# Inter-chunk products of a Mamba-style scan as 64x64 quarter products on an unpadded state

## What is computed

```python
def step(state, inp):
    x_t, b_t, c_t, dt_t = inp
    decay = jnp.exp(dt_t * a)[..., None, None]
    b_bar = dt_t[..., None] * b_t
    state = decay * state + b_bar[..., None] * x_t[:, :, None, :]
    y_t = jnp.einsum('bhn,bhnp->bhp', c_t, state)
    return (state, y_t)
...
b = (x @ Wb.T).reshape(bsz, seq, HEADS, STATE)
c = (x @ Wc.T).reshape(bsz, seq, HEADS, STATE)
dt = jax.nn.softplus(x @ Wdt.T + b_dt)
y = _ssd_scan(xh, b, c, dt, a)
y = y + d_param[None, None, :, None] * xh
```

## Time and profile before

| | us |
|---|---|
| median of 3 runs | 1465.38 |
| lowest, highest | 1464.57, 1468.33 |
| the profiled execution | 1465.41 |
| its span in the trace | 1463.4 |
| TensorE busy | 1403.8 (96%) |
| VectorE busy | 996.6 (68%) |
| granted TensorE clock, mean | 0.988 |

### The profile page before, as it was taken

The page is one execution under the profiler, slowest core; times in us unless marked ns, Lnnn a source line. Parts: engine busy times, 40 slices in busy tenths (PEclk is TensorE's granted clock), DMA queues, the critical chain, the costliest instruction groups (busy, mean ns, idle before and its releaser), DMA issues.

```text
span 1463.4 us, 23472 instructions
## 1 busy us (share of the span) xinstructions
PE 1403.8 (96%) x8803; PEld 862.6 (59%) x8803; DVE 996.6 (68%) x2849; ACT 689.1 (47%) x1351; POOL 308.5 (21%) x386
## 2 busy tenths in 40 slices
PE   8999999999999999999999999999999997999984
PEld 4447645676457665576456764576655763567543
DVE  2426797477874787477974778747874779747682
ACT  4443543645455562635436454555626354462312
POOL 3004201341104301142013411043011420133110
PEclk9999999999999999999999999999999998999998
DMA  8000001020000100020010200001000200101010
GB/s 299 10 0 30 15 15 48 3 75 29 26 23 17 61 30 26 22 78 15 15 48 2 76 30 26 22 18 61 29 26 22 77 15 15 47 4 46 29 48 4
DMA packets 47552, 54.24 MB, mean 37 GB/s; under 512 B 7625, under 2 KB 42313, under 8 KB 47441
## 3 DMA queue, kind: packets, MB, share of 16 engines
q1 hardware_dynamic: 41424, 46.41, 9.5%
q0 software_dynamic: 6016, 6.35, 1.7%
HBM read 34.84 MB, written 17.85 MB: 36 GB/s over the span
## 4 chain that ended last, share of the span: by engine, by line
PE 85%; DVE 8%; issue 4%; ACT 1%; POOL 1%; DMA 0%; POOLq 0%; SPq 0%; DVEq 0%
PE ps L1563 41%; PE ps L1729 8%; PE ps L1678 5%; PE ps L1637 4%; PE ps L1630 4%; DVE yst L1166 3%; PE ps L1690 2%; PE ps L1649 2%; PE ps L1869 2%; PE ps L1879 2%; PE ps L1664 2%; PE ps L1655 2%; PE ps L1668 1%; PE ps L1834 1%; PE ps L1800 1%
## 5 line engine op out<-in xcount | busy, mean ns | idle before, releaser
L1563 PE MATMUL ps<-xT,wb_s 128*128 128x512 f32 x512 | 232.9, 601 | 3.6 <-ACT xT L722 3.5
L1563 PE MATMUL ps<-xT,wc_s 128*128 128x512 f32 x512 | 225.4, 593 | 0.0
L1563 PEld LDWEIGHTS ps<-xT,wc_s 128*128 128x128 f32 x512 | 96.1, 190 | 112.3 <-issue 111.9
L1563 PEld LDWEIGHTS ps<-xT,wb_s 128*128 128x128 f32 x512 | 94.1, 191 | 113.1 <-issue 104.5
L1047 DVE SCALAR_TENSOR_TENSOR xT<-xc,cols_s,xT 128x512 f32<-128x512 f32 x192 | 134.8, 748 | 2.7
L1563 PE MATMUL ps<-hT,wx_s 128*128 128x512 f32 x256 | 117.7, 603 | 1.6 <-ACT hT L680 1.2
L1563 PE MATMUL ps<-hT,wz_s 128*128 128x512 f32 x256 | 112.8, 593 | 0.1
L1729 PE MATMUL ps<-CT,xT 128*128 128x256 f32 x512 | 111.9, 379 | 0.9 <-DVE xT L1226 0.9
L747 ACT ACTIVATE BT<-ps 128x512 f32<-128x512 f32 x64 | 37.9, 592 | 150.4 <-PE ps L1563 150.4
L1729 PEld LDWEIGHTS ps<-CT,xT 128*128 128x128 f32 x512 | 97.2, 190 | 17.8 <-issue 5.0
L788 ACT ACTIVATE XB<-ps 128x512 f32<-128x512 f32 x64 | 38.3, 599 | 138.0 <-PE ps L1649 138.0
(11 more groups left out here) (299 smaller groups left out, 2637.5 us busy)
## 6 DMA issues: line engine op xcount, KB each, us to landing
xr<-x SPq DMA_DIRECT2D x8, 1024.0 KB, 9.2
x_scratch<-xr SPq DMA_DIRECT2D x32, 256.0 KB, 2.1
out<-EC SPq DMA_DIRECT2D x32, 256.0 KB, 2.1
BT<-x SPq DMA_DIRECT2D x7, 1024.0 KB, 5.6
modrow<-mod_scratch SPq DMA_DIRECT2D x8, 512.0 KB, 6.6
w_s<-w SPq DMA_DIRECT2D x2, 1024.0 KB, 11.5
BT<-x SPq DMA_DIRECT2D x2, 512.0 KB, 5.2
xT<-wmod SPq DMA_DIRECT2D x1, 1024.0 KB, 9.4
```

The costliest lines, as they stand in the source:

```text
L1563: ins = t_.matmul(bank[:, :], w[:, k, m * P:(m + 1) * P], rhs[:, k, half * HALF:(half + 1) * HALF], start=k == 0, stop=k == nk - 1)
```

## The change

- The state is kept without its zero quarters: `Sst` is 128 partitions by 4 tiles by 64 columns. The inter-chunk product becomes 8 products of 64 rows by 64 columns, each 128 tokens long.
- In tiles 1 and 3 the two heads' state rows are swapped: head `hh` of an odd tile has its state rows in the other half of the partitions. So the quarter products of an even tile go from rows 0 to 63 to output partitions 0 to 63, and from 64 to 127 to 64 to 127; those of an odd tile cross over. The swap of B, C and dt is made in the order of the weights that the host passes.
- y lies in two banks: even tiles in bank 4, columns 0 to 255, odd tiles in bank 5, columns 256 to 511. The state's own products use columns 0 to 255 of bank 5.
- Since y and the state's products share bank 5, TensorE's `state(c)` also waits for `y_ready`, and VectorE's `state(c)` waits for `y_filled` in chunk 0 too.
- VectorE's `state` is one instruction of 128 partitions by 256 instead of two of 64 by 256. GpSimd's decay works on 128x256 instead of 128x512. Two memsets of VectorE per sequence and two of GpSimd in the setup are gone.

```diff
+        def y_tile(k, rows=slice(0, P)):
+
+            o = (k % 2) * 2 * P + (k // 2) * P
+            return ps[4 + k % 2][rows, o:o + P]
...
-        Sbd = sb("Sbd", [P, KC, P])
-        Sdc = sb("Sdc", [P, KC, P])
+        Sst = sb("Sst", [P, KC, STATE])
+        Sdc = sb("Sdc", [P, KC, STATE])
...
-                    g.tensor_tensor(Sdc[:, :, :], Sbd[:, :, :], dec[:, :, c:c + 1].broadcast_to([P, KC, P]),
+                    g.tensor_tensor(Sdc[:, :, :], Sst[:, :, :], dec[:, :, c:c + 1].broadcast_to([P, KC, STATE]),
...
                 def state(c):
                     dve.wait_ge(s_filled, at(s_filled, b, c + 1))
                     if c:
-                        if c or later(b):
-                            dve.wait_ge(Sdc_ready, at(Sdc_ready, b, c))
-
-                        dve.wait_ge(y_filled, at(y_filled, b, c + 1))
-                    for hh in range(2):
-                        q = slice(64 * hh, 64 * hh + 64)
-                        src = ps[5][q, :].rearrange("p (k n) -> p k n", k=KC)[:, :, q]
-                        if c:
-                            ins = v.tensor_tensor(Sbd[q, :, q], src, Sdc[q, :, q], ALU.add)
-                        else:
-                            ins = v.tensor_copy(Sbd[q, :, q], src)
+                        dve.wait_ge(Sdc_ready, at(Sdc_ready, b, c))
+                    dve.wait_ge(y_filled, at(y_filled, b, c + 1))
+                    src = ps[5][:, 0:HALF // 2].rearrange("p (k n) -> p k n", k=KC)
+                    if c:
+                        ins = v.tensor_tensor(Sst[:, :, :], src, Sdc[:, :, :], ALU.add)
+                    else:
+                        ins = v.tensor_copy(Sst[:, :, :], src)
...
-                v.memset(Sbd[0:64, 0, 64:128], 0.0)
-                chS(dve, b, v.memset(Sbd[64:128, 0, 0:64], 0.0))
...
                     for k in range(KC):
-                        t_.matmul(ps[4][:, k * P:(k + 1) * P], Sbd[:, k, :], ECv[:, k, c * P:(c + 1) * P],
-                                  start=k == 0, stop=True, skip_group_check=k > 0)
+                        for r in range(2):
+                            q = slice(64 * r, 64 * r + 64)
+                            hh = (r + k) % 2
+                            t_.matmul(y_tile(k, slice(64 * hh, 64 * hh + 64)), Sst[q, k, :],
+                                      ECv[q, k, c * P:(c + 1) * P], start=k < 2, stop=True,
+                                      skip_group_check=k >= 2)
...
                     if c or later(b):
                         pe.wait_ge(S_ready, at(S_ready, b, c))
-                    for h in range(HEADS):
-                        r, o = slice(64 * (h % 2), 64 * (h % 2) + 64), slice(h * 64, h * 64 + 64)
-                        ins = t_.matmul(ps[5][r, o], XB[:, c % 2, 1, o], XB[:, c % 2, 0, o], start=True, stop=True)
+                        pe.wait_ge(y_ready, at(y_ready, b, c))
+                    for k in range(KC):
+                        for r in range(2):
+                            hh = (r + k) % 2
+                            o, x = k * P + 64 * r, k * P + 64 * hh
+                            ins = t_.matmul(ps[5][64 * r:64 * r + 64, k * STATE:(k + 1) * STATE],
+                                            XB[:, c % 2, 1, o:o + STATE], XB[:, c % 2, 0, x:x + STATE],
+                                            start=True, stop=True)
```

More of the change, by code:

```diff
@@ L44 @@
 SD_MOD, SD_MIX, SD_ALL = 11, 13, 17
-SP_ALL = 46
+SP_ALL = 44
 DT_FLOOR = 2.0 ** -60
-CHAINS = {"A": 4, "V": 9, "D": 7, "S": 4, "G": 20, "R": 45}
+CHAINS = {"A": 4, "V": 9, "D": 7, "S": 3, "G": 20, "R": 45}
 PER_BATCH = {}
@@ L266, in adaln_block @@
         vz = ftmp[:, 3:5, :].rearrange("p a n -> p (a n)").rearrange("p (h n) -> p h n", h=FH)
-        msel = Sbd[:, 0, :]
+        msel = Sst[:, 0:2, :].rearrange("p a n -> p (a n)")
         junk = oT_
@@ L547, in _ @@
             link(g.memset(phase[:, 1, 1, :], PI / 2))
-            link(g.memset(Sbd[:, :, :], 0.0))
-            link(g.memset(Sdc[:, :, :], 0.0))
             link(g.memset(boff[:, :], 0.0))
@@ L1158, in skip @@
                         s = xT[:, k, c * P:(c + 1) * P]
-                        ins = v.scalar_tensor_tensor(s, s, cols_s[:, k, 5:6], ps[4][:, k * P:(k + 1) * P],
-                                                     ALU.mult, ALU.add)
+                        ins = v.scalar_tensor_tensor(s, s, cols_s[:, k, 5:6], y_tile(k), ALU.mult, ALU.add)
                     ins.then_inc(y_ready, 1)
@@ L1636, in output @@
                     k, hh = h // 2, h % 2
-                    ins = t_.matmul(ps[4][64 * hh:64 * hh + 64, k * P:(k + 1) * P],
+                    r = (hh + k) % 2
+                    ins = t_.matmul(y_tile(k, slice(64 * hh, 64 * hh + 64)),
                                     XB[:, c % 2, 0, h * STATE:(h + 1) * STATE],
-                                    Mt[:, c % 2, hh * HALF + k * P:hh * HALF + (k + 1) * P],
+                                    Mt[:, c % 2, r * HALF + k * P:r * HALF + (k + 1) * P],
                                     start=c == 0, stop=True, skip_group_check=c > 0)
@@ L2018 @@
     rep = INNER // HEADS
+    heads = [2 * k + (r + k) % 2 for k in range(KC) for r in range(2)]
+    states = np.concatenate([np.arange(h * STATE, (h + 1) * STATE) for h in heads])
     columns = np.concatenate([
@@ L2025 @@
         "x": arr("L0_attn_input_tensor"),
-        "wxT": arr("L0_attn_Wx").T, "wzT": arr("L0_attn_Wz").T, "wbT": arr("L0_attn_Wb").T,
-        "wcT": arr("L0_attn_Wc").T, "wdtT": np.pad(arr("L0_attn_Wdt").T, ((0, 0), (0, 32 - HEADS))),
+        "wxT": arr("L0_attn_Wx").T, "wzT": arr("L0_attn_Wz").T, "wbT": arr("L0_attn_Wb")[states].T,
+        "wcT": arr("L0_attn_Wc")[states].T,
+        "wdtT": np.pad(arr("L0_attn_Wdt")[heads].T, ((0, 0), (0, 32 - HEADS))),
         "woT": arr("L0_attn_Wout").T, "cols": by_partition(columns),
-        "bdt": np.tile(np.pad(arr("L0_attn_b_dt"), (0, 32 - HEADS)), 4)[:, None], "loga": arr("L0_attn_log_a"),
+        "bdt": np.tile(np.pad(arr("L0_attn_b_dt")[heads], (0, 32 - HEADS)), 4)[:, None],
+        "loga": arr("L0_attn_log_a")[heads],
         "mask": arr("L0_ffn_attention_mask").reshape(MB * L, L),
```

## The result

| | us |
|---|---|
| forecast | 1441.0 (1438 to 1457) |
| measured, median of 4 runs | 1443.74 (1441.15 to 1446.76) |
| before, median of 4 runs beside them | 1465.54 (1464.57 to 1468.33) |
| ratio, with 95% interval | 0.985 (0.983 to 0.988) |
| the same kernel again, 5 more runs (first experiment) | 1441.69 (1439.80 to 1445.84) |

The profiled execution is the slowest of the four: 1446.76, span 1444.9. So between the two traces the difference is 18.5, and between the medians 21.8 and 24.0.

A forecast was written before the change was run, and what follows sets the result against it. TensorE was taken to bound the scan, its matmul groups abutting for a whole chunk. 48 x 0.50 = 24.0 plus VectorE's 0.4 gave 24.4 off 1465.41, so 1441.0 us, range 1438 to 1457.

The forecast's parts named there:

- The length of the group: TensorE's inter-chunk product: 4 turns (0.43) plus a fixed part of 0.16 give 0.59 us instead of 1.09.
- Four side by side: In the inter-chunk product the array takes four quarter passes at once, 0.50 us less per group; chance 0.72.
- Two wide: Rival for the inter-chunk product: 8 turns, 1.02 us per group, gain 3.8, total 1461.6; chance 0.13.
- How often it counts: Inter-chunk products of chunks 1 to 6 are on the chain: 48 of 56, 24.0 us; chunk 7's count nothing.
- VectorE's 0.44, once: VectorE's `state` goes from 0.86 to 0.42; the 0.44 comes out only in the last sequence, where TensorE waits 1.12.
- The added waits: TensorE's `state(c)` on `y_ready` (0.85 ahead at `state(5)`) and VectorE's copy in chunk 0: cost nothing.
- GpSimd: GpSimd's L572 halves from 1.05, with 129 us of idle ahead of it and 1% of the chain: nothing gained.
- The idle ahead of the group-norm matmul: Sign at the end of each scan: TensorE's idle ahead of gn_stats' matmul grows from 0.25 to about 0.75.
- cutting it only adds 0.50: Cutting `output(7)`, beside VectorE's statistics, adds 0.50 to TensorE's idle of 0.25 and gains nothing in all 8 sequences.
- The sum: Whole kernel: 24.0 from TensorE plus 0.4 from VectorE is 24.4, from 1465.41 to 1441.0 us.

The follow-up runs named there:

- first experiment: The changed kernel run again with no edit, as a control: median 1441.69 us, 0.983 of the kernel before.
- second set: Changed kernel with the inter-chunk products of chunks 1 to 6 issued twice, one set right behind the other: 1464.99 us, 0.998 of the kernel before.
- the two doublings: Changed kernel with inter-chunk products issued twice, in chunks 1 to 6 (1464.99 us, 0.998 of before) or in chunk 7 alone (1441.35 us, 0.982).
- a trace that starts and ends as the one before: Trace of the changed kernel with only chunk 7's inter-chunk products issued twice: span 1439.4, median 1441.35 us, 0.982 of the kernel before.

## Why the prediction was right, point by point

- **The length of the group.** Forecast 0.59, measured 0.60. The reading of the earlier trace rows, that a group is so many turns of 0.108 plus a fixed part, held, and it held in the other forms that ran: 8 turns 1.02, two times 4 turns 1.03 (second set 0.43 = 4 x 0.108).
- **Four side by side.** That no row showed a cut in rows and columns at once was the largest open point; the sum took four, and four it was. "Two wide", a gain of 3.8, is what the kernel without the swap gave: 2.4 in the median (1463.28 against 1465.66), and 3.4 in its trace from the mark of sequence 0 to that of sequence 7.
- **How often it counts.** 48 and not 56: shown by the two doublings.
- **VectorE's 0.44, once.** The last sequence gave 3.5, of which 2.94 are TensorE's. The rest is 0.54, not 0.44. The rows of the kernel after (compare):

```profile
1325.81 0.43 DVE L1148 TENSOR_TENSOR Sst<-ps,Sdc 128x256 f32<-128x256 f32 x1 [2.02 <-PE ps L1638]
1326.15 1.11 DVE L1158 SCALAR_TENSOR_TENSOR xT<-xT,cols_s,ps 128x128 f32<-128x128 f32 x4
...
1327.32 0.67 PE L1629 MATMUL ps<-EC,Sst 64*64 64x128 f32 x16 [0.56 <-DVE xT L1158]
```

  and of the kernel before the row behind its `state` at 1345.53:

```profile
1346.42 1.12 DVE L1159 SCALAR_TENSOR_TENSOR xT<-xT,cols_s,ps 128x128 f32<-128x128 f32 x4
```

  The forecast set the lengths of the rows against each other, 0.86 and 0.42. What counts is when skip can start: 0.89 behind `state` before (1346.42 - 1345.53) and 0.34 after (1326.15 - 1325.81), 0.55 less. So the wait fell from 1.12 to 0.56 and not to 0.7. What the sum did not say either is that the shorter instruction keeps the added wait from biting in the other sequences: with it in two instructions, 0.18 of a period is lost.
- **The added waits.** Nothing, as forecast, but the margin was put at 0.85 and is 1.1. The 0.11 by which VectorE's saving was too small counts twice in it.
- **GpSimd.** Nothing, as forecast. Its decay did not halve from 1.05 (it takes 0.62), but it is off the chain.
- **The idle ahead of the group-norm matmul.** Forecast "about 0.75", measured 0.55. The step that failed is "cutting it only adds 0.50": `output(7)` did not become 0.50 shorter. TensorE's timeline before (two rows that the forecast did not use) and after:

```profile
666.19 1.98 PE L1563 MATMUL ps<-hT,wx_s 128*128 128x512 f32 x4
...
669.00 1.09 PE L1637 MATMUL ps<-Mt,XB 128*64 128x128 f32 x16
```

```profile
658.20 1.98 PE L1559 MATMUL ps<-hT,wx_s 128*128 128x512 f32 x4
660.11 0.67 PE L1629 MATMUL ps<-EC,Sst 64*64 64x128 f32 x16
660.71 1.09 PE L1638 MATMUL ps<-Mt,XB 128*64 128x128 f32 x16
```

  From the projection ahead of it to the intra-chunk product it was 669.00 - 666.19 = 2.81 and is 2.51: 0.30 less, which takes the idle from 0.25 to 0.55. The padded product took only 0.99 there (668.01 to 669.00), not 1.09, and the quarters start 0.09 later than it did (1.91 after the projection's start instead of 1.82). A reading that fits, not tested by itself: ahead of `output(7)` stands a full 128x128 matmul, the padded product had that shape too, and the quarters change it; in the loop the neighbour ahead has 64 columns, so both forms pay for a change. It costs nothing here since the place is beside VectorE.
- **The sum.** 1441.0 against 1443.74 and 1441.69. Of the 24.4, a trace that starts and ends as the one before shows 24.0 (1463.4 to 1439.4): 48 x 0.49 + 0.55 = 24.1. Two small errors stood against each other, 0.50 for 0.49 and 0.44 for 0.55. What the forecast left out is that the start and the last feed-forward part vary from one execution to the next; in the profile of the changed kernel they lost 3.7 and 1.8.

## What to carry to other kernels

A product on a block-diagonal operand uses the array for zeros. Cutting it helped here only because the pieces land on different row and column parts of the array at once; arranging the data so that every second tile crosses over (here by permuting weights ahead of time) was worth 0.42 of 0.49 us per chunk's group, and the cut alone 0.07. Price an instruction of VectorE by the distance to the start of the next one, not by the length of its row. Price a group of matmuls as turns of the array plus a fixed part, both read from neighbours in the same trace, and count only those places where the chain of waits runs through TensorE.

When a change shortens one engine's work, look at which idle it leaves on that engine and whether work of the other can be moved into the other's idle: the statistics moved by one and two chunks gave another 0.8 us per sequence.

## What was not expected of the hardware

- The order of the eight quarter products in the program is nearly free: 0.61 against 0.60 us when the first four use two quarters and the last four the other two.
- Two row halves of the array write different partitions of one PSUM bank side by side: 16 passes in 0.60 us on four quarters, of which two always write bank 4 and two bank 5.
- At 11 us into the program six bf16 passes took 1.46 in one execution and 2.72 in another, and the table by stretch shows a granted clock of 1.00 for both (first before, then after). In these first microseconds the length of a known pass told of the loss, and the column did not.

```profile
4.00:16.00 12.00, 10.85 (x47) 6.37 (x48) 4.45 (x23) 6.08 (x12) 6.33 (x25) 1.00 0.97 337
```

```profile
4.00:19.00 15.00, 14.74 (x47) 8.99 (x48) 4.45 (x23) 6.34 (x12) 9.04 (x32) 1.00 1.01 355
```
